# Layer 2's softmax: exponentials on ScalarE per head and tile, straight from PSUM, with the negated maximum as bias

## The reference

```python
qkv = (x @ w_qkv).reshape(b, n, 3, H, hd).transpose(2, 0, 3, 1, 4)
q, k, v = (qkv[0], qkv[1], qkv[2])
attn = jnp.einsum('bhnd,bhmd->bhnm', q, k) * scale
attn = jnp.where(attn_mask[None, None] == 0, -jnp.inf, attn)
attn = jax.nn.softmax(attn, axis=-1)
o = jnp.einsum('bhnm,bhmd->bhnd', attn, v).transpose(0, 2, 1, 3).reshape(b, n, d)
```

## Time and profile before

| | us |
|---|---|
| median of three runs | 1381.44 |
| lowest and highest | 1379.06, 1381.63 |
| the profiled execution's own time | 1379.5 |
| its span, first to last instruction | 1377.7 |
| PE busy | 1345.8 (98%) |
| DVE busy | 1113.5 (81%) |
| ACT busy | 784.8 (57%) |

### The profile page before, as it was taken

The page is one execution under the profiler, slowest core; times in us unless marked ns, Lnnn a source line. Parts: engine busy times, 40 slices in busy tenths (PEclk is TensorE's granted clock), DMA queues, the critical chain, the costliest instruction groups (busy, mean ns, idle before and its releaser), DMA issues.

```text
span 1377.7 us, 27138 instructions
## 1 busy us (share of the span) xinstructions
PE 1345.8 (98%) x10460; PEld 1141.8 (83%) x10460; DVE 1113.5 (81%) x2441; ACT 784.8 (57%) x1444; POOL 135.1 (10%) x194
## 2 busy tenths in 40 slices
PE   8999999999999999999999999999999999999996
PEld 8888878888888888888888888888888888888785
DVE  6889878788888879788887888879888787869555
ACT  3455656556665665656556565665656456654544
POOL 4010111010010100001010000101001010101000
PEclk9999999999999999999999999999999999999998
DMA  5000010100000001010100000000000100100100
GB/s 178 9 17 24 1 25 31 24 30 15 8 30 23 30 15 38 0 23 30 23 30 15 23 15 23 30 23 31 12 11 30 23 32 1 39 9 1 46 0 31
DMA packets 54671, 34.54 MB, mean 25 GB/s; under 512 B 34912, under 2 KB 51552, under 8 KB 54624
## 3 DMA queue, kind: packets, MB, share of 16 engines
q1 hardware_dynamic: 52816, 29.43, 7.2%
q0 software_dynamic: 1248, 3.94, 0.9%
q10 hardware_dynamic: 560, 0.52, 0.1%
HBM read 12.92 MB, written 8.39 MB: 15 GB/s over the span
## 4 chain that ended last, share of the span: by engine, by line
PE 89%; DVE 7%; ACT 2%; issue 1%; DMA 0%; POOLq 0%; DVEq 0%; POOL 0%; ACTq 0%
PE banks L122 22%; PE banks L124 21%; PE banks L123 21%; PE banks L667 8%; PE banks L662 3%; PE banks L937 3%; PE banks L826 2%; PE banks L841 2%; PE banks L743 2%; PE banks L815 2%; ACT l_htok L1468 1%; PE banks L804 1%; PE banks L1036 1%; DVE l_r L2522 0%; PE banks L735 0%
## 5 line engine op out<-in xcount | busy, mean ns | idle before, releaser
L1604 ACT ACTIVATE l_r<-banks,bias_r 128x512 f32<-128x512 f32 x90 | 61.4, 682 | 177.4 <-PE banks L124 177.3
L264 POOL TENSOR_TENSOR l_rstd<-l_mv,eps 128x4 f32<-128x4 f32 x47 | 19.2, 409 | 908.6 <-DVE l_mv L258 908.6
L1468 ACT ACTIVATE l_rh_hi<-l_r 128x512 fp32r<-128x512 f32 x90 | 56.4, 627 | 62.1 <-DVE l_r L2511 61.9
L1621 ACT ACTIVATE banks<-banks,bias_h 128x512 f32<-128x512 f32 x96 | 63.4, 662 | 25.4 <-PE banks L124 25.0
L122 PE MATMUL banks<-l_rh_hi,u_hi 128*128 128x512 f32 x180 | 76.1, 423 | 0.1
L1615 ACT ACTIVATE banks<-banks,bias_z 128x512 f32<-128x512 f32 x96 | 63.5, 663 | 19.7 <-PE banks L124 19.7
L278 ACT ACTIVATE y<-l_sum,l_offset,l_rstd 128x256 f32<-128x256 f32 x124 | 69.1, 598 | 6.1 <-DVE l_offset L272 6.0
L124 PE MATMUL banks<-l_rh_lo,u_hi 128*128 128x512 f32 x180 | 71.1, 395 | 0.0
L123 PE MATMUL banks<-l_rh_hi,u_lo 128*128 128x512 f32 x180 | 70.7, 393 | 0.0
L667 PE MATMUL banks<-adj_t,y 128*128 128x128 f32 x544 | 68.1, 277 | 1.5 <-DVE l_otok L2460 1.5
L1537 ACT ACTIVATE l_qk<-banks 128x512 f32<-128x512 f32 x64 | 38.3, 598 | 54.1 <-PE banks L124 53.4
(11 more groups left out here) (308 smaller groups left out, 4418.2 us busy)
## 6 DMA issues: line engine op xcount, KB each, us to landing
x_tok<-in_x_dram SPq DMA_DIRECT2D x15, 512.0 KB, 3.5
l_res<-y SPq DMA_DIRECT2D x15, 512.0 KB, 2.9
out_dram<-l_res SPq DMA_DIRECT2D x15, 512.0 KB, 2.9
l_vpair<-l_vstage SPq DMA_DIRECT2D x32, 128.0 KB, 3.0
w_raw<-in_L_gnn_w_w_dram POOLq DMA_DIRECT2D x3, 512.0 KB, 7.5
qkv_raw<-in_L_gnn_w_qkv_dram POOLq DMA_DIRECT2D x1, 768.0 KB, 4.5
l_res<-in_x_dram SPq DMA_DIRECT2D x1, 512.0 KB, 5.4
u_raw<-in_L_gnn_u_w_dram POOLq DMA_DIRECT2D x2, 256.0 KB, 7.4
```

The lines of the kernel that those rows point to most:

```text
L1468: return nc.scalar.activation(out, source, ACT.Copy)
L1604: nc.scalar.activation(own(u).r[:, m, :], rz(u)[:, m, :], ACT.Tanh, scale=0.5, bias=w.biases["r"][:, m:m + 1]).then_inc(s.r_ready.of(u), 1)
L1621: nc.scalar.activation(hv(u)[:, m, :], hv(u)[:, m, :], ACT.Tanh, bias=w.biases["h"][:, m:m + 1]).then_inc(s.hv_ready.of(u), 1)
```

## The change

ScalarE reads the scores from PSUM and computes exp(score - maximum) in one instruction, with the maximum, negated by VectorE, as the bias. A bias is one number per partition, and each head and tile has its own maximum, so there is one instruction per head and tile: 8 of 128x64 for each of the four banks, 32 per unit. They are issued bank by bank, those of bank r behind the maximum of bank r. The four shifts of VectorE are gone, and with them their signal. The signal of the exponentials now counts banks: each bank touches all four tiles, so every sum waits for the fourth bank. The places of `l2_exp` in ScalarE's lists stay where they were; its second argument is now the bank instead of the tile.

```diff
-        self.l2_scored, self.l2_maxed, self.l2_shifted = one("l2_scored", ROWS), one("l2_maxed", ROWS), one("l2_shifted", ROWS)
-        self.l2_exp, self.l2_prob_turned, self.l2_prob_t = one("l2_exp", TILES), one("l2_prob_turned", TILES), one("l2_prob_t", TILES)
+        self.l2_scored, self.l2_maxed = one("l2_scored", ROWS), one("l2_maxed", ROWS)
+        self.l2_exp, self.l2_prob_turned, self.l2_prob_t = one("l2_exp", ROWS), one("l2_prob_turned", TILES), one("l2_prob_t", TILES)
...
-        def l2_exp(u, t):
-            if t == 0:
-                act.wait_ge(*s.l2_shifted.at(u, ROWS))
-            nc.scalar.activation(b.prob[:, t, :, :], b.prob[:, t, :, :], ACT.Exp).then_inc(s.l2_exp.sem, 1)
+        def l2_exp(u, r):
+
+            act.wait_ge(*s.l2_maxed.at(u, r + 1))
+            if is_second(u) and r == 0:
+                act.wait_ge(*s.l2_prob_turned.at(0, TILES))
+            for t in range(TILES):
+                for c in range(CH):
+                    q = t * CH + c
+                    ins = nc.scalar.activation(b.prob[:, t, c * ROWS + r, :], front(u)[:, r, q * NODES:(q + 1) * NODES], ACT.Exp,
+                                               bias=b.mx[:, r, q:q + 1])
+            ins.then_inc(s.l2_exp.sem, 1)
...
-                                    AX.X, ALU.max).then_inc(s.l2_maxed.sem, 1)
-
-        @within
-        def l2_shift(u, r):
-            dve.wait_ge(*s.l2_maxed.at(u, r + 1))
-            if is_second(u):
-                dve.wait_ge(*s.l2_prob_turned.at(0, TILES))
-            by_bank = b.prob[:, :, :, :].rearrange("p t (c r) j -> p t c r j", c=CH)
-            m = b.mx[:, r, :].rearrange("p (t c) -> p t c", t=TILES).unsqueeze(3).to_broadcast([P, TILES, CH, NODES])
-            nc.vector.tensor_tensor(by_bank[:, :, :, r, :], front(u)[:, r, :].rearrange("p (t c j) -> p t c j", t=TILES, c=CH),
-                                    m, ALU.subtract).then_inc(s.l2_shifted.sem, 1)
+                                    AX.X, ALU.max, negate=True).then_inc(s.l2_maxed.sem, 1)
 
         @within
         def l2_sum(u, t):
-            dve.wait_ge(*s.l2_exp.at(u, t + 1))
+            dve.wait_ge(*s.l2_exp.at(u, ROWS))
...
             l2_max(i + 1, 2)
-            l2_shift(i + 1, 0)
-            l2_shift(i + 1, 1)
             l2_max(i + 1, 3)
-            l2_shift(i + 1, 2)
-            l2_shift(i + 1, 3)
             l3_reset(i, 0, 0)
             l2_sum(i + 1, 0)
```

More of the change, by code:

```diff
@@ L2777, in fill @@
             l1_residual(1, 0)
-            l2_shift(0, 0)
             l2_max(0, 3)
             l1_residual(1, 1)
-            for n in range(1, 4):
-                l2_shift(0, n)
             for n in range(2):
@@ L2835, in fill @@
                 l2_max(1, n)
-            l2_shift(1, 0)
             for n in range(2):
@@ L2840, in fill @@
             l2_max(1, 3)
-            l2_shift(1, 1)
             f_low_a(0, 1)
-            for n in range(2, 4):
-                l2_shift(1, n)
             l0_statistics(2)
@@ L2954, in drain @@
                 l2_max(13, n)
-            l2_shift(13, 0)
             for n in range(2, 4):
                 l2_max(13, n)
-            for n in range(1, 4):
-                l2_shift(13, n)
             l3_variance(11)
@@ L3063, in drain @@
                 l2_max(14, n)
-            l2_shift(14, 0)
             l2_max(14, 3)
-            for n in range(1, 4):
-                l2_shift(14, n)
             l3_reset(13, 0, 0)
@@ L3135, in drain @@
                 l2_max(15, n)
-            for n in range(4):
-                l2_shift(15, n)
             for n in range(2):
```

## The result

| | before | after |
|---|---|---|
| median (lowest to highest), us | 1379.86 (1379.06 to 1381.63), 5 runs | 1488.51 (1488.02 to 1489.29), 5 runs |
| the profiled execution | 1379.5 | 1488.7 |
| its span | 1377.7 | 1486.9 |
| mean granted clock of TensorE | 0.994 | 0.963 |

The ratio is 1.078, with a 95% interval from 1.0771 to 1.0795. The forecast was 1491.

A forecast was written before the change was run, and what follows sets the result against it. TensorE, busy 98% of the span, was taken as the bound, with the softmax arriving just in time. Loop stalls 63.8, other units 21.7 and clock 26 sum to 111.5 on 1379.5: 1491 us, range 1455 to 1530.

The forecast's parts named there:

- loop, stall before the transposes: In each of 11 loop passes TensorE stalls 5.8 us before the transposes, 63.8 us in all.
- stalls of units 0, 1, 13, 14, 15: Outside the loop: unit 0 loses 6.0 us, units 1, 13 and 15 3.7 each, unit 14 4.6; together 21.7.
- behind the stalls: TensorE's clock falls in each of 16 stalls and returns late, costing 1.6 us each, 26 us in all.
- The bound: In the loop the softmax reaches TensorE's transposes just in time, slack 0.1 us; delaying the first sum by more stalls TensorE.
- The small exponential: On ScalarE, 128x64 exponentials start 200 ns apart; the last one's own duration is 300 ns.
- (a): Rival: the small exponential costs up to 330 ns, 58 us more, so 1549; chance 0.13, in part or whole.
- (b): Rival: the small exponential costs only 120 ns, 36 us less, so 1455; chance 0.09.
- The sums wait for the fourth bank: In the loop all sums wait for the fourth bank's exponentials and start 5.9 us later.
- Rival (d): The clock costs nothing because VectorE sets the work behind the stall; 26 us less, so 1465; chance 0.09.
- rival (c): The clock stays low through transposes and `l2_attend`, 3.4 us lost per stall instead of 1.6, so 1520; chance 0.12.
- Rival (e): VectorE's queue is the real pace, so the 64 removed shifts, 38 us, come off: 1341; chance 0.01.

The follow-up runs named there:

- Experiment 3: The kernel before, with one wait changed: every sum waits for all four exponentials instead of its own; 1408.48 us, ratio 1.0208.
- experiment 1: Changed kernel plus 30 identity transposes by TensorE in each loop pass, issued once the exponentials are done; 1474.46 us, ratio 1.0681.
- Experiment 7: Changed kernel with one bias and one exponential per bank, exponentials moved ahead of the Tanh (unit 0: copies) in every unit, sums moved earlier too; 1373.10 us, ratio 0.9949.
- experiments 4: Changed kernel with one maximum and one 128x512 exponential per bank, 4 instructions in place of 32, at their old places; 1406.35 us, ratio 1.0186.
- experiment 8: Kernel before, shifts and four large exponentials kept, with exponentials ahead of the Tanh (unit 0: copies) and sums ahead of layer 3's product; 1394.71 us, ratio 1.0103.
- experiments 9: Changed kernel, 32 exponentials per unit kept, all four banks ahead of the Tanh in every unit, sums ahead of layer 3's product; 1424.72 us, ratio 1.0322.
- Experiment 2: Changed kernel with the exponentials of banks 0, 1 and 2 ahead of the Tanh in ScalarE's loop list; 1442.45 us, ratio 1.0448.
- 6: Changed kernel with one 128x128 exponential per tile and bank, both heads sharing a bias, 16 instructions per unit instead of 32; 1443.69 us, ratio 1.0456.

## Why the prediction was right, by its own steps

| term | predicted | measured, after less before |
|---|---|---|
| loop, stall before the transposes | 11 x 5.8 = 63.8 | 11 x 5.77 = 63.4 |
| stalls of units 0, 1, 13, 14, 15 (forecast in the order 0, three alike, 14) | 6.0 + 3 x 3.7 + 4.6 = 21.7 | 6.96 + 3.81 + 3.55 + 4.36 + 3.71 = 22.4 |
| behind the stalls (forecast as clock) | 26 | 15.1 in the loop, 7.4 outside = 22.5 |
| sum | 111.5 | 108.3, of a span difference of 109.2 |

- **The bound.** "The softmax arrives just in time: its slack is 0.1 us" was the step that carried the rest. Experiment 3 tests it alone: sums 1.56 us later cost 1.57 a pass. So there is no slack in effect: TensorE started the transposes 0.15 later than the first product would have let it, but the last product sets their end. "Less the slack of 0.1" was the slip in this step, 0.16 x 11 = 1.8 us. (The 0.69 us that the prediction gave one product is its recorded duration, not a quarter of the row of 2.50, which is 0.62; the end of the first product, 610.98, is right.)
- **The small exponential.** 200 ns from start to start, taken from the Tanh less 448 columns, was 196. Rivals (a), 330, and (b), 120, fall with it. The Trainium skill ("ScalarE: Activation LUTs", section "What ACT_TABLE_LOAD costs") has a formula for an instruction with one pointer operand, and 240 ns is the estimate by it for 64 columns back to back; the trace is 18% under that. What was off is the duration of one, 0.30 expected; the group's row has this:

```profile
L1562 ACT ACTIVATE l_prob<-banks,l_mx 128x64 f32<-128x64 f32 x512 | 107.2, 424 | 5.2 <-DVE l_mx L2421 5.2
```

  A mean of 424 ns, for instructions that start 196 apart: records overlap, and only the distance counts. The record of the last one is 6.64 - 31 x 0.196 = 0.56 us, 0.26 more than was forecast. That the stall still came out right to 0.1 is luck in part: the 31 distances were 0.12 shorter in sum, and the first exponential started 0.58 behind the Tanh instead of 0.66.
- **The sums wait for the fourth bank.** Right: the last exponential ends at 750.33 and the sums start at 750.36.
- **Units 0 and 14.** 6.0 expected and 7.0 measured in unit 0. The start of the sums was right to 0.3 (they began 5.7 later, 75.72 against 70.01), but the prediction followed only the softmax to L826. TensorE stopped earlier, at L725, for the step of layer 0 behind the sums in VectorE's list. In unit 14 it was the same: 2.81 of the 4.4 us stand at L122, where TensorE waited for a Tanh (L1611) that is queued behind the 32 exponentials.
- **Where the idle time stands.** 85 us before L826 was forecast; it is 72.4 there, with 7.2 at L725 and 2.8 at L122 for the other two, 82.4 together. TensorE's share is 92%, not 90%, and VectorE lost 36 us of work, not 41.
- **The clock.** Right in sign, right in size to 3.5 us, and partly by luck. The low stretch is 3.4 us, as in the earlier trace rows, in five passes of the loop and 6.8 us, twice that, in the other six. But some of it lies in the hole itself, and the first transposes behind it are paced by VectorE's products, so the clock cost 1.2 a pass where 1.6 was forecast; the other 0.16 of the row is the slack that was wrongly taken off above. Rival (d), that it costs nothing, and rival (c), 3.4 a pass, both fall; experiment 1 takes the clock's cost out of the loop and gets 14 us back.
- **Rival (e)**, VectorE as the real pace: it lost 36 us of work in the changed kernel, and the time rose. Experiment 7 drops the shifts too and gains 8 us, none of it by VectorE's total: the waits of TensorE there are those of before, and what shortened was a stretch in which VectorE's products had set the pace of 16 transposes.

## What to carry to other kernels

Before work is taken from an engine with 81% of busy time, ask who waits for it: here 38 us of subtraction lay, in the loop, behind another engine's wait, and the 28 instructions put in their place, about 0.14 us each on top of their columns, lay on a path without slack. A per-partition operand that changes every 64 columns is expensive on ScalarE for that reason, and cutting by bank what the reader takes by tile adds a second loss, since every reader then waits for the last piece. When such a path does get shorter, move what stands in front of it and behind it in each in-order list as well, and move it only where the wait that it used to fill is gone too: the same order took 2.4% off one kernel (experiments 4 and 7, 1406.35 and 1373.10) and cost 1% in another (experiment 8).

## What the runs showed of the hardware that was not expected

How long TensorE stood idle in the loop, and in how many of the passes with that idle time the clock was down behind it (tail over 5 us instead of 4.41). In unit 2 of experiments 9 and 2 TensorE was idle for 0.26 and 0.71 only, and the clock stayed up:

| run | idle before L826, us | passes with a lower clock |
|---|---|---|
| 3 and 4 | 1.25, 1.38 | none |
| 9 | 2.00 | 7 of 10 |
| 2 | 2.10 | 8 of 10 |
| 6 | 3.19 | 6 of 11 |
| changed kernel | 5.61 | 11 of 11 |

The same hole brings the clock down in one pass and not in the next. Experiment 2, TensorE before a tail of 4.41 (unit 5) and three windows: the first behind that hole, the second behind the hole of unit 7 with a tail of 5.53, the third around the hole of unit 13, where TensorE was idle for 3.74 us before 1155.33:

```profile
471.10 2.46 PE L826 MATMUL banks<-ident,l_prob 128*128 128x128 f32 x16 [2.10 <-DVE l_prob L2445]
```

```profile
471.00:476.00 5.00, 4.90 (x82) 4.07 (x83) 4.09 (x13) 3.17 (x6) 1.88 (x2) 1.00 0.00 0
641.00:647.00 6.00, 5.74 (x81) 5.35 (x82) 4.25 (x13) 2.89 (x6) 1.56 (x2) 0.72 0.00 0
1151.00:1162.00 11.00, 7.26 (x95) 6.05 (x94) 8.70 (x17) 5.83 (x12) 0.00 (x0) 1.00 0.01 1
```

Between about 2 and 3.7 us of idleness it was thus a matter of the pass, and within that range a longer hole did not make it surer. What decides it in a pass is open; no run told that apart. Nor had the recorded durations of short instructions been expected to mislead: L1562 is listed with a mean of 424 ns, as if 32 took 13.6 us, and they took 6.6.
